# Cross attention of a fused attention and expert kernel: k, x, q and mask rows prepared two batches early, single PSUM banks for the maxima, double ones for the exponentials

## The reference, cut to what matters

```python
x = x + _L0_xattn_ref(_layernorm(x), ctx_1024, ctx_1024)
x = x + _L0_ffn_ref(_layernorm(x), gate_w, gate_up_proj, down_proj)
x = x + _L1_xattn_ref(_layernorm(x), ctx_1024, ctx_1024, mask, Wq, bq, Wk, bk, Wv, bv, Wo, bo)
x = x + _L1_ffn_ref(_layernorm(x), Wq, Wkv, Ws, Wo, bo)

def _L1_xattn_ref(Q, K, V, mask, Wq, bq, Wk, bk, Wv, bv, Wo, bo):
    q, k, v = heads(Q @ Wq.T + bq), heads(K @ Wk.T + bk), heads(V @ Wv.T + bv)
    scores = einsum('bhqd,bhkd->bhqk', q, k) / sqrt(16)
    scores = where(mask[:, None] == 0, -1e9, scores)
    out = einsum('bhqk,bhkd->bhqd', softmax(scores), v)
    return merged(out) @ Wo.T + bo
```

## Time and profile before

| what | us |
| --- | --- |
| median of 3 runs (lowest, highest) | 2673.34 (2672.87, 2675.73) |
| the profiled execution | 2665.32 |
| its span, from the first instruction to the last | 2663.6 |
| busy: PE, DVE, ACT, POOL | 2122.1, 1484.3, 926.3, 836.8 |
| cross attention, from its first transfer (L760) to the first of the next stage (L1218) | 998.4 to 1692.1 |
| mean granted clock of PE | 0.937 of full speed |

### The profile page before, as it was taken

One profiled execution on the slowest core, in us unless ns is written; L12 is line 12 of the kernel. 1 busy time (PEld: TensorE's weight loads), 2 busy tenths in 40 slices (PEclk: granted clock), 3 DMA queues, 4 the chain that ended last, 5 costly groups with the idle time before them and its releaser, 6 DMA issues. The chain is left out here.

```text
span 2663.6 us, 37640 instructions
## 1 busy us (share of the span) xinstructions
PE 2122.1 (80%) x11952; PEld 1389.3 (52%) x11961; DVE 1484.3 (56%) x2297; ACT 926.3 (35%) x1539; POOL 836.8 (31%) x753
## 2 busy tenths in 40 slices
PE   2340899999999505889888888838999999999997
PEld 1340899999999502333333333614545545554554
DVE  7820454545554344567666666544656656656655
ACT  2410333333333200455555555312333333333332
POOL 0067553435550362122212222011323323333232
PEclk9999999999999856899999999669999999999999
DMA  3162332333322332232232232324233223223322
GB/s 126 63 243 101 111 115 79 117 122 110 122 78 65 109 88 88 89 102 89 82 104 84 87 98 86 118 53 95 58 73 86 65 68 86 69 61 86 76 56 64
DMA packets 149071, 244.68 MB, mean 92 GB/s; under 512 B 22502, under 2 KB 71310, under 8 KB 146698
## 3 DMA queue, kind: packets, MB, share of 16 engines
q1 hardware_dynamic: 109762, 164.07, 21.9%
q0 software_dynamic: 11104, 44.06, 4.8%
q10 hardware_dynamic: 28160, 35.99, 4.2%
HBM read 120.48 MB, written 67.04 MB: 70 GB/s over the span
## 5 line engine op out<-in xcount | busy, mean ns | idle before, releaser
L1108 DVE TENSOR_REDUCE ca_negmax<-ca_na 128x2 f32<-128x1024 f32 x272 | 332.4, 1224 | 153.6 <-PE ca_na L901 153.6
L1020 ACT ACTIVATE ca_pr<-ca_st 128x512 f32<-128x512 f32 x512 | 278.9, 597 | 206.6 <-PE ca_st L915 205.6
L901 PE MATMUL ca_na<-ca_k_stack,ca_q_stack 64*128 64x512 f32 x544 | 222.7, 489 | 59.0 <-DMA ca_q_stack<-ca_zrow 55.6
L592 DVE TENSOR_TENSOR ex_h<-ex_up,ex_sg 128x512 f32<-128x512 f32 x136 | 94.1, 692 | 306.8 <-ACT ex_sg L555 197.4
L1706 DVE TENSOR_REDUCE sa_negmax<-sa_na 128x1 f32<-128x512 f32 x272 | 182.7, 674 | 130.8 <-PE sa_na L1527 126.5
L915 PE MATMUL ca_st<-ca_q_stack,ca_k_stack 64*128 64x512 f32 x512 | 210.6, 473 | 29.5 <-ACT ca_pr L1020 26.5
L515 PE MATMUL ex_gp<-ex_xp,moe_gu_p 128*128 128x256 f32 x1632 | 221.8, 286 | 1.4 <-DVE ex_xp L578 1.4
L515 PE MATMUL ex_up<-ex_xp,moe_gu_p 128*128 128x256 f32 x1632 | 218.4, 284 | 0.0
L528 PE MATMUL ex_yp<-moe_dn_p,ex_hp 128*128 128x256 f32 x1632 | 208.8, 286 | 11.3 <-DVE ex_hp L582 11.3
L515 PEld LDWEIGHTS ex_gp<-ex_xp,moe_gu_p 128*128 128x128 f32 x1632 | 206.1, 193 | 2.4 <-DVE ex_xp L578 1.8
L528 PEld LDWEIGHTS ex_yp<-moe_dn_p,ex_hp 128*128 128x128 f32 x1632 | 198.8, 192 | 15.2 <-DVE ex_hp L582 15.2
(11 more groups left out here) (261 smaller groups left out, 3798.1 us busy)
## 6 DMA issues: line engine op xcount, KB each, us to landing
sa_q<-sa_qh SPq DMA_DIRECT2D x140, 128.0 KB
sa_k<-sa_kh SPq DMA_DIRECT2D x140, 128.0 KB
ex_raw_m<-masks ACTq DMA_DIRECT2D x34, 512.0 KB, 3.8
moe_gu_raw<-gateupT POOLq DMA_DIRECT2D x8, 2048.0 KB, 8.2
ca_q_stack<-q_parts SPq DMA_DIRECT2D x216, 64.0 KB
ca_k_stack<-k_parts SPq DMA_DIRECT2D x216, 64.0 KB
expert_rows<-rt_zeros SPq DMA_DIRECT2D x20, 512.0 KB, 15.9
k_parts<-ca_kp SPq DMA_DIRECT2D x9, 1024.0 KB, 4.3
```

The costliest lines, as they stand in the source:

```text
L901: last = pe.matmul(na[r % 2][:, i, :], q_stack[g][rows, i, t * P:(t + 1) * P], k_stack[g][rows, i, :], start=not masked, stop=True)
L1020: act.activation(pr[:, s // HG % 2, s % HG, :], st[s % 2][:, :], ACT.Exp, scale=DK ** -0.5).then_inc(exp_done, 1)
L1108: dve.tensor_reduce(negmax[:, g % 2, 1 - r % 2, :, r // 2], na[r % 2][:, :, :], AX.X, ALU.max, negate=True).then_inc(max_done, 1)
```

## The change

The job table is written anew: unit 0 has m, n0, xT0, t0, xT1, t1; unit 1 has m, v0, n1, o0, v1, rv; unit 2 m, k0, n2, o1, k1; unit 3 m, q0, n3, q1. xT, rv, k and q are now those of the batch after the next; v is still that of the next. The mask rows `nbT` have three buffers, and the context a second copy `ctxK`, which k reads. `FIRST` prepares x, mask, k and q of batches 0 and 1. On SP, both stores stand at the end of the loop's body, after `load_stack(3)` and a wait until all four stacks have landed; two bias transfers and two context transfers stand at the start of the body, ahead of `send_rows(1, ...)`. `na` becomes two single banks with one reduction of 128 x 512 per slot, `st` two double banks with one exponential of 128 x 1024 per run. The semaphores count accordingly.

```diff
+        ctxK = m.sb("ctxK", [P, KC, S])
-        nb, nbT = m.sb("nb", [P, 2, TB, S], BF16), m.sb("nbT", [P, 2, TB, S], BF16)
+        nb, nbT = m.sb("nb", [P, 2, TB, S], BF16), m.sb("nbT", [P, 3, TB, S], BF16)
-        na = [m.ps(f"na{i}", [P, 2, S]) for i in range(2)]
-        st = [m.ps(f"st{i}", [P, S]) for i in range(2)]
+        na = [m.ps(f"na{i}", [P, S]) for i in range(2)]
+        st = [m.ps(f"st{i}", [P, 2, S]) for i in range(2)]
-        JOBS = [("m", 0, 0), ("k0", 0, 1), ("n0", 0, 2), ("k1", 0, 3), ("xT0", 0, 4), ("xT1", 0, 5), ("rv", 0, 6), ("q0", 0, 7),
...
+        JOBS = [("m", 0, 0), ("n0", 0, 3), ("xT0", 0, 4), ("t0", 0, 5), ("xT1", 0, 6), ("t1", 0, 7),
+                ("m", 1, 0), ("v0", 1, 1), ("n1", 1, 2), ("o0", 1, 3), ("v1", 1, 5), ("rv", 1, 7),
...
-        FIRST = ["k0", "k1", "xT0", "xT1", "rv", "q0", "q1", "v0", "v1", "m"]
+        FIRST = [("k0", 0), ("k1", 0), ("xT0", 0), ("xT1", 0), ("rv", 0), ("q0", 0), ("q1", 0), ("v0", 0), ("v1", 0),
+                 ("xT0", 1), ("xT1", 1), ("rv", 1), ("k0", 1), ("k1", 1), ("q0", 1), ("q1", 1), ("m", 0)]
@@ block.sync, before the loop
+            load_context(sp, io, ctxK, ck_in, 1)
+            load_bias_T(0, 0)
+            load_bias_T(1, 1)
             load_bias(0, 0)
...
             for g in range(G):
                 load_stack(g)
-            sp.wait_ge(misc_full, FIRST.index("v1") + 1)
-            load_context(sp, io, ctxT, ctx_in, 1)
+            for g in range(G):
+                sp.wait_ge(stack_in[g], LOAD)
+            store(kp, k_parts, misc_free, k_stored, first("k1", 1) + 1)
+            store(qp, q_parts, qp_ready, q_stored, 2 * KC)
             send_rows(0, 0)
             with sp.Fori(0, B) as b:
-                sp.wait_ge(exp_done, b * G * SLOTS + 2)
-                for g in range(G):
-                    sp.wait_ge(stack_in[g], b * LOAD + LOAD)
-                load_bias(nxt(b), (b + 1) % 2)
-                send_rows(1, b * G + 1)
-                store(kp, k_parts, misc_free, k_stored, b * nj + (nf + number("k1") + 1))
-                send_rows(2, b * G + 2)
-                store(qp, q_parts, qp_ready, q_stored, b * KC + 2 * KC)
+                sp.wait_ge(exp_done, b * G * RUNS + 2)
+                load_bias((b + 1) % B, (b + 1) % 2)
+                load_bias_T((b + 2) % B, (b + 2) % 3)
+                load_context(sp, io, ctxT, ctx_in, (b + 1) % B)
+                load_context(sp, io, ctxK, ck_in, (b + 2) % B)
+                send_rows(1, b * G + 1)
                 for g in range(G):
-                    sp.wait_ge(exp_done, b * G * SLOTS + ((g + 1) * SLOTS + 2))
+                    sp.wait_ge(exp_done, b * G * RUNS + ((g + 1) * RUNS + 2))
                     if g == 0:
                         sp.wait_ge(k_stored, b * 16 + 32)
                         sp.wait_ge(q_stored, b * 16 + 32)
                     load_stack(g)
-                    if g == 1:
-                        send_rows(3, b * G + 3)
-                    if g == 2:
-                        load_context(sp, io, ctxT, ctx_in, (b + 2) % B)
-                        send_rows(0, b * G + 4)
+                    if g < G - 1:
+                        send_rows((g + 2) % G, b * G + (g + 2))
+                for g in range(G):
+                    sp.wait_ge(stack_in[g], b * LOAD + 2 * LOAD)
+                store(kp, k_parts, misc_free, k_stored, b * nj + (nf + number("k1") + 1))
+                store(qp, q_parts, qp_ready, q_stored, b * KC + 3 * KC)
@@ score_a
-                if i == 0:
-                    pe.wait_ge(max_done, a * RUNS + r + 1)
+                pe.wait_ge(max_done, a * SLOTS + s + 1)
@@ score_b
-                pe.wait_ge(exp_done, u * SLOTS + s + 1)
+                if i == 0:
+                    pe.wait_ge(exp_done, u * RUNS + r + 1)
@@ the exponential on ACT
-                            act.activation(pr[:, s // HG % 2, s % HG, :], st[s % 2][:, :], ACT.Exp, scale=DK ** -0.5).then_inc(exp_done, 1)
+                        act.activation(pr[:, r // 2 % 2, 2 * (r % 2):2 * (r % 2) + 2, :], st[r % 2][:, :, :], ACT.Exp,
+                                       scale=DK ** -0.5).then_inc(exp_done, 1)
@@ DVE: maximum, and normalise in the loop
-                dve.wait_ge(na_full, a * RUNS + r + 1)
-                dve.tensor_reduce(negmax[:, g % 2, 1 - r % 2, :, r // 2], na[r % 2][:, :, :], AX.X, ALU.max, negate=True).then_inc(max_done, 1)
+                for i in range(2):
+                    dve.wait_ge(na_full, a * SLOTS + (2 * r + i + 1))
+                    dve.tensor_reduce(negmax[:, g % 2, 1 - r % 2, i, r // 2:r // 2 + 1], na[i][:, :], AX.X, ALU.max, negate=True).then_inc(max_done, 1)
...
-                        if (g, r) == (0, 1):
-                            normalise(b + 1, (b + 1) % B)
+                        if (g, r) == (0, 0):
+                            normalise(b + 2, (b + 2) % B)
```

More of the change, by code:

```diff
@@ L751, in number, with first, batch @@
             return next(n for n, j in enumerate(JOBS) if j[0] == name)
-        def nxt(b):
-            return b + 1 if isinstance(b, int) else (b + 1) % B
+        def first(name, b):
+            return FIRST.index((name, b))
+        def batch(name, b):
+            return b + 1 if name[0] == "v" else b + 2
         @block.sync
@@ L786, in send_rows @@
                                      mrow[j * 2 * TB:(j + 1) * 2 * TB, r, :].bitcast(F32)).then_inc(m_in, 16)
+            load_context(sp, io, ctxK, ck_in, 1)
+            load_bias_T(0, 0)
+            load_bias_T(1, 1)
             load_bias(0, 0)
             sp.wait_ge(set_up, SETUP)
-            store(kp, k_parts, misc_free, k_stored, FIRST.index("k1") + 1)
+            store(kp, k_parts, misc_free, k_stored, first("k1", 0) + 1)
             store(qp, q_parts, qp_ready, q_stored, KC)
@@ L867, in prepare @@
                 if name == "rv":
-                    pe.wait_ge(nbT_in, b * 16 + 16)
+                    pe.wait_ge(nbT_in, 32 if isinstance(b, int) else b * 16 + 16)
                     for t in range(TB):
-                        last = pe.matmul(misc[:, :], tiny16[:, :], nbT[:, b % 2, t, :], start=(t == 0), stop=(t == TB - 1))
+                        last = pe.matmul(misc[:, :], tiny16[:, :], nbT[:, b % 3, t, :], start=(t == 0), stop=(t == TB - 1))
                 elif name[0] == "k":
-                    pe.wait_ge(ctx_in, b * 16 + 16)
+                    now = isinstance(b, int) and b == 0
+                    if now:
+                        pe.wait_ge(ctx_in, 16)
+                    else:
+                        pe.wait_ge(ck_in, b * 16)
                     for i in range(KC):
-                        last = pe.matmul(misc[:, :], wk[:, i, c * P:(c + 1) * P], ctxT[:, i, :], start=(i == 0), stop=(i == KC - 1))
+                        last = pe.matmul(misc[:, :], wk[:, i, c * P:(c + 1) * P], (ctxT if now else ctxK)[:, i, :], start=(i == 0), stop=(i == KC - 1))
                 elif name[0] == "x":
@@ L882, in prepare @@
                 else:
+                    pe.wait_ge(ctx_in, b * 16 + 16)
                     for t in range(2):
@@ L896, in score_a @@
                         pe.wait_ge(nb_in, b * 16 + 16)
-                if i == 0:
-                    pe.wait_ge(max_done, a * RUNS + r + 1)
+                pe.wait_ge(max_done, a * SLOTS + s + 1)
                 if masked:
[L900 to L904, removed]
+                    pe.matmul(na[i][:, :], ident16[:, :], nb[:, b % 2, t, :], start=True, stop=False)
+                pe.matmul(na[i][:, :], q_stack[g][rows, i, t * P:(t + 1) * P], k_stack[g][rows, i, :],
+                          start=not masked, stop=True).then_inc(na_full, 1)
             def score_b(g, b, s, u, masked):
-                t, i, j = s // HG, s % 2, s // 2 % 2
+                r, t, i, j = s // 2, s // HG, s % 2, s // 2 % 2
                 rows = slice(j * HALF, (j + 1) * HALF)
@@ L958, in all_units @@
                                 else:
-                                    prepare(job, name, b + 1)
+                                    prepare(job, name, batch(name, b))
             pe.wait_ge(w_in, 16 * 8)
-            for n, name in enumerate(FIRST[:-1]):
-                if n == 0:
-                    pe.wait_ge(set_up, SETUP)
-                prepare(n, name, 0)
+            pe.wait_ge(set_up, SETUP)
+            for n, (name, b) in enumerate(FIRST[:-1]):
+                prepare(n, name, b)
             for t in range(TB - 1):
@@ L972, in _ @@
                 all_units(False)
[L973 removed]
+            pe.wait_ge(exp_done, B * G * RUNS + 2)
             values(G - 1, TB - 1)
@@ L1008, in _ @@
             act.wait_ge(set_up, SETUP)
-            for n, name in enumerate(FIRST):
+            for n, (name, b) in enumerate(FIRST):
                 if name[0] in "kxm":
-                    evacuate(n, name, 0)
+                    evacuate(n, name, b)
             with act.Fori(0, B) as b:
@@ L1075, in _ @@
             for c in range(KC):
```

(22 more changed lines are left out.)

43 lines of the change are left out of this document (23 added, 20 removed), and 5 rows, old and new, of the table JOBS.

## The result

The changed kernel took 2714.16 us (median of 4 runs, 2706.87 to 2721.26) beside 2674.53 for the kernel before (4 runs, 2672.87 to 2679.33): a ratio of 1.0147, 95% interval 1.0118 to 1.0176. The forecast was 2698, slower. The profiled execution took 2721.26, its span 2719.5, at a mean granted clock of 0.928; it is the longest of the four (2706.87, 2707.79, 2720.53, 2721.26).

A forecast was written before the change was run, and what follows sets the result against it. PE was taken as nearest to the bound, idling mainly for a late stack load. Terms +17 - 9.3 + 7 x 2.0 + 3 = +24.7 on 2665.3 gave 2690, or 2698 against the median; range 2669 to 2717, widened 2652 to 2722.

The forecast's parts named there:

- the sum: Whole kernel: prologue +17, batch 0 -9.3, seven batches at +2.0 each, end +3, together +24.7 us.
- first job to the loop: Prologue: seven more jobs in FIRST start the loop 10 to 19 us later, taken as +17.
- batch 0: First batch: no load_stack(3) or store, so no wait for rows; 69.5 us against 78.8, -9.3.
- batches 1 to 7: Loop: each batch takes 77.0 us against 75.0, so 7 x 2.0 more.
- end: After the last unit: load 3, both stores and their landing take 17 us against 14.1, +3.
- The removed wait: Unit 2's start: PE's wait for load_stack(0) goes, with its slow clock, -8.8 us a batch.
- The new wait: Unit 1's start: PE waits 7.8 us for the rows of maxima, then 3.0 us of half clock.
- landing at +23.3: Rows for unit 1, issued behind 4.2 MB, land 23.3 us after unit 0's start; PE arrives at +15.5.
- 0.4 for the rows themselves: Part of the landing: 0.4 us for unit 1's rows after the 4.2 MB ahead of them.
- rival 1: Unit 1's rows not held behind 4.2 MB, 1.2 us to land: 2639 to 2660; break-even landing +19.8; chance 0.15.
- The walk of PE's order: PE's 32 runs by unit: 66.5 us a batch with 7.6 of waits, +0.3 against 66.2 before.
- Rival 3: Single banks bind PE to DVE: 3.0 us more a batch in units 1 to 3, 2719; chance 0.12.

The follow-up runs named there:

- the wait before `load_stack(0)`: The changed kernel with SP made to wait for the landing of unit 1's rows before it issues load_stack(0): 2696.99 us, ratio 1.0104.
- rows behind the stores only: The changed kernel with unit 1's rows issued ahead of the bias and context transfers, still behind both stores: 2637.66 us, ratio 0.9896.
- the rows first: The changed kernel with unit 1's rows issued ahead of the context, both stores and the bias on SP's queue: 2615.1 us, ratio 0.9808.
- the repeat: The changed kernel timed once more without an edit, beside the later runs: 2717.53 us, ratio 1.0142.
- the early jobs: The kernel with the rows first, with k0, k1, q0, q1 of batch 1 moved inside the first pass of score products: 2618.65 us, ratio 0.9787.

## Why the prediction was right, point by point

The medians differ by 39.6 us, the sum said 24.7: the direction is right, and more than a third of the size is missing. The profiled executions differ by 55.9, since before's is 9.2 below its median and the changed one's 7.1 above; they are compared here by the sum's terms. A batch ends where the next would start.

| term | predicted | measured |
| --- | --- | --- |
| ahead of the cross attention | 0 | +7.2 |
| first job to the loop | +17 | 85.7 - 66.3 = +19.4 |
| batch 0 | -9.3 | 67.8 - 78.4 = -10.6 |
| batches 1 to 7 | +14 | 560.3 - 525.8 = +34.5 |
| end | +3 | 16.8 - 13.7 = +3.2 |

The rest, 2.4, is behind the cross attention.

**The removed wait** went as said: its row is gone, and unit 2 takes 17.60.

**The new wait** is where it was put, for the reason given; two experiments on its place in the queue show it. **Mis-sized was its length, "landing at +23.3"**: PE goes on at +25.8 in batch 4 and at +26.1 on average. The 4.2 MB were not under-rated: the sum has them through at +22.9, and the rows' packets are through at +22.7; with the wait before `load_stack(0)`, where nothing else moves, the last packet of the bulk starts at +22.9. Mis-sized was "0.4 for the rows themselves". It covers their packets, which took 0.4, but not the time from the last packet until PE goes on, 3.2 us here. Where next to nothing moves behind them, that time is 1.2 (rows behind the stores only) and 1.4 (the wait before `load_stack(0)`); the rest goes with the packets of `load_stack(0)`, since with that wait the rows came 2.1 earlier. The sum's rival 1 did count 1.2 to land. PE reached unit 1 at +15.2, 0.3 before the sum. The late landing makes 2.8 x 7 = 20 of the 20.5 us missed in the batches. Three falls of the clock in unit 3 are 4.5 more, and unit 1, at 20.0 on average with its half clock, gives 3.4 back against the 20.5 allowed.

**The walk of PE's order** gave 15.5, 17.8, 17.7 and 15.5. With the rows first, the units measure 15.12, 17.84, 17.59 and 15.65. Its sum, 66.5, was right. The comparison with before, "+0.3", has no run to show it: before's 66.2 was worked out by taking the wait and its clock away on paper. Old banks with the new order and all transfers in time measure 64.9 in batches 1 to 7, so the new banks cost 1.3 us a batch, 1.9 where the clock is full. Rival 3 named DVE's single banks rightly and priced them at 3.0 a batch. The measured 2714.16 is nearer to its 2719 than to 2698, but not by its cause: PE's waits for `ca_negmax` are 4.3 us from 1000 to 1740, and the missing time is in the landing.

**How much of the hit is luck.** The forecast's own upper end, 2717, allowed 1 us for a later landing, and it was 2.8 later. By the terms, without the 7.2 ahead of the cross attention, the profiled execution lost 24 us more than counted; added to 2698 that is 2722, the very end of the range. The median lies well inside because two of the four times are 14 us shorter.

**Rival 1** put a break-even at +19.8 for the landing, 7 us of time for each us. The kernel behind the stores only, with PE going on at +17.1, had a ratio of 0.9896, on the faster side as that says, and the rows on ACT's queue, with +20.5, one of 1.0027. On SP's queue the landings came in the order of issue, though the rows' packets moved beside the last of the bulk; on ACT's queue alone did the rows overtake.

**The prologue** lay near its upper bound. It goes with the clock: from the first job to the first `score_a` it took 60.5 here and 60.3 in the repeat, both at 0.67, but 58.4 at 0.70 and 55.0 at 0.78 in two kernels with the same prologue (the wait before `load_stack(0)` and the rows behind the stores only). **Batch 0 and the end** came as counted.

## What to carry to other kernels

A small transfer that an in-order engine needs soon belongs ahead of the bulk on its queue, and its landing is to be counted with what is ahead of it and with what is issued right behind. Here 16 KB of rows moved ahead of 4.2 MB were worth 90 us, and turned a change for the worse into one that beats both kernels. A change made of several parts should be timed in parts: two-batches-early preparation pays once the rows are in time, while the banks that came with it cost 10 to 17 us in both surroundings.

## What was not expected

- An issue does not always cost its issuer the same: three took ACT 3.35 us where the one before took 0.65, and ACT stood idle 3.40 us before its next exponential. With the rows behind the stores only, SP took 4.48 us for the four, 1.4 for each of the middle two. Full DMA engines alone do not explain it, since in the changed kernel SP issues the four in 2.78 us with the engines as full, and in 2.74 with the rows first, when little else moves. Both slow cases lie 2 to 5 us behind the issue of the stores; the cause is open.
- The clock falls to 0.50 in unit 3 of some batches though PE waits for nothing there longer than 0.2 us, at a cost of 1.5 us each time: in three of seven batches of the changed kernel, one of the repeat, one with the early jobs, two with the rows behind the stores only, all seven with the wait before `load_stack(0)`, and none of the other kernels. What sets it off stays open.
- With the old banks PE's weight loads wait 13.7 us a batch for ACT, and the batch is still 1.1 us shorter than with 5.0 and 3.3 us for DVE and ACT: waits of the weight loader can lie beside running matmuls, so their sum is no measure of what banks cost.
